# A dense table streamed by one transfer of 128 KB per step into a ring of eight, instead of 512 KB per four steps into a ring of four

## The chip, the cores and the metric

The kernel runs on one core of one Trainium2 chip. The metric is the device time of a run in microseconds. PE is TensorE, DVE is VectorE, ACT is ScalarE, POOL is GpSimd, and SP is the sync engine, which here does nothing but issue transfers.

## The reference, cut to what matters

The model is a token mixer, a gated recurrent layer in both directions, and then a product-key attention over 16 sequences (batches) of 375 positions. Only the last stage touches the change. There, each position scores two lists of 64 keys per head, keeps 16 of each, takes the best 16 of their sums out of 4096 combinations, and sums the 16 chosen rows of a table with softmax weights:

```python
sim = jnp.einsum('pbnhd,pkhd->pbnhk', q, pk_keys)
scores, idx = jax.lax.top_k(sim, PK_TOPK)
...
final_scores, pk_idx = jax.lax.top_k(score, FINAL_TOPK)
final_scores = jax.nn.softmax(final_scores, axis=-1)
...
k = jnp.einsum('bnhk,bnhkd->bnhd', kv_scores, keys_table[ind])
v = jnp.einsum('bnhk,bnhkd->bnhd', kv_scores, values_table[ind])
```

A causal attention with these k and v and an output projection follow. Everything is float32 at the outputs.

## The kernel before, in words

The first 1090 us hold the mixer, the recurrence and its output. The rest is `attention` (line 740). It treats four heads by gathering: POOL issues 3024 indirect transfers of 128 rows (line 937), and PE sums the rows. The other four heads (DH = 4) are dense: the weights of all 4096 combinations are made on the chip and multiplied with the whole table. A batch is STEPS = 64 steps, 16 per dense head, and a step handles two chunks of 128 table rows:

- `exponent` (line 987): PE forms the exponents of 2 x 128 rows by 375 positions in banks 0 and 1, and ACT takes the exponential into `ex` (line 1203);
- `ranks` (line 1012): PE forms the sums that tell whether a row is chosen, and DVE compares and multiplies into `w` (line 1526);
- `product` (line 1020): PE multiplies two 128 x 128 tiles of the table, `dtab`, with `w`, adding in bank 4. In float32 each of the two shows as two weight loads and two matmuls in the trace, so a product is four of each.

PE's order within a step is written out in `step` (line 1107): the exponents of the next step, the product of the step before, the ranks of the next step, then other work by a table of places (`places`, line 656): attention scores, gathered rows, transposes. DVE, ACT and POOL run their own orders, tied to PE's by semaphores. All of it stands in one loop over batches 1 to 14, with batch 0 and 15 written out before and behind it (`run`, line 833).

The dense table in HBM holds 2 MB per head, 8 MB in all, and is read again for every batch. `dtab` (line 770) is a ring of SLOTS = 4 buffers of PIECE = 8 chunks, 4 KB per partition each, 16 KB in all; a piece is 512 KB and serves four steps. In the program of SP (line 888), `piece` (line 892) issues one such transfer, and `batch` (line 901) waits on `s_main`, which counts finished products, until the four steps of a buffer are done, and then refills it. SP has two other waits on the same queue: at a batch's start `h_now` (lines 902 and 903) waits for the promotion of the next rows (`s_cur`), and `row` (lines 905 and 906) waits for the fourth exponent of the batch (`s_X`); the store of the output of the batch before (line 909) comes between pieces. On PE, the product of every fourth step waits for its piece (line 1022) and, as all products do, for `w` (line 1023).

Which wait goes with which piece is a matter of three expressions:

```python
SLOTS = 4; PIECE = 8                                     # chunks in a piece
sp.wait_ge(s_main, n * STEPS + 4 * (i + 1))              # line 911, i in 0..15
pe.wait_ge(s_piece[p // 4 % SLOTS], n * (16 * DH) + 16 * (p // 4 // SLOTS + 1))   # line 1022
```

Of the kernel before, what the change touches and what calls it, by code (L numbers as in the profile page):

```python
# [15 lines left out]
T = (T_IN - 1) // STRIDE + 1  # L16
# [25 lines left out]
DH = H - GH  # L42
CHUNKS = NK * NK // 128
HALF = CHUNKS // 2
STEPS = DH * HALF
PIECE = 8
SLOTS = 4
HEADS = NT * H
LEN = 15

# [689 lines left out]
def attention(nc, cst, keymat, halves, table, dense, minus, hu, out, ps):  # L740
# [10 lines left out]
    with ExitStack() as ctx:  # L751
        BF16 = mybir.dt.bfloat16

        def sb(name, shape, dt=F32):
            return ctx.enter_context(nc.sbuf_tensor(name, shape, dt))

        def sem(name):
            return ctx.enter_context(nc.semaphore(name))
# [10 lines left out]
        left = sb("left", [128, 2, T])  # L769
        dtab = sb("dtab", [128, SLOTS, PIECE * 128])  # L770
        half = sb("half", [128, HALVES_WIDTH], BF16)
        ex = sb("ex", [128, 2, 2, T])
        w = sb("w", [128, 2, 2, T])
# [41 lines left out]
        s_row, s_h = sem("c_rows_loaded"), sem("c_residual_loaded")  # L815
        s_piece = [sem(f"c_piece_loaded{i}") for i in range(SLOTS)]
        s_cur = sem("c_row_promoted")
        s_X, s_D, s_ex, s_w, s_main, s_acc = (sem(n) for n in ("d_exponent", "d_rank_sum", "d_exp", "d_weight", "d_product", "d_head_copied"))
# [68 lines left out]
        @block.sync  # L887
        def _(sp):
            def row(b):
                sp.dma_start(u_front[0:64, :], hu[1, bass.ds(b, 1)].rearrange("o d t -> (o d) t")).then_inc(s_row, 16)  # L890

            def piece(i):
                h, part = i // 4, slice((i % 4) * PIECE * 128, (i % 4 + 1) * PIECE * 128)
                sp.dma_start(dtab[:, i % SLOTS, :], dense[h, :, part]).then_inc(s_piece[i % SLOTS], 16)

            def store(n):
                sp.wait_ge(s_osb, n)
                dst = out[bass.ds(n - 1, 1)].rearrange("o (c t) d -> t (o c) d", c=NT)
                sp.dma_start(dst, osb[:]).then_inc(s_out, 16)

            def batch(n, kind):
                sp.wait_ge(s_cur, n + 1)
                sp.dma_start(h_now[:], hu[0, bass.ds(n, 1)].rearrange("o d t -> (o d) t")).then_inc(s_h, 16)
                if kind != "last":
                    sp.wait_ge(s_X, n * STEPS + AHEAD)
                    row(n + 1)
                for i in range(4 * DH):
                    if i == 11 and kind != "first":
                        store(n)
                    if not (kind == "last" and i + SLOTS >= 4 * DH):  # L910
                        sp.wait_ge(s_main, n * STEPS + 4 * (i + 1))
                        piece((i + SLOTS) % (4 * DH))

            sp.dma_start(kdup[64:68], minus.rearrange("r h (j k) -> r h j k", j=2)).then_inc(s_kdup, 16)
            row(0)
            for i in range(SLOTS):
                piece(i)
            batch(0, "first")
            with sp.Fori(0, B - 2) as i:
                batch(i + 1, "mid")  # L920
            batch(B - 1, "last")
            store(B)
            sp.wait_ge(s_out, 16 * (B + 1))
# [19 lines left out]
        def _(pe):  # L943
            def mm(out_, lhsT, rhs, start=True, stop=True, open_bank=False):
                return nc.tensor.matmul(out_, lhsT, rhs, start=start, stop=stop, skip_group_check=open_bank)  # L945
# [72 lines left out]
                last.then_inc(s_D, 1)  # L1018

            def product(n, p):  # L1020
                if p % 4 == 0:
                    pe.wait_ge(s_piece[p // 4 % SLOTS], n * (16 * DH) + 16 * (p // 4 // SLOTS + 1))
                pe.wait_ge(s_w, n * STEPS + (p + 1))
                if p % HALF == 0:
                    pe.wait_ge(s_acc, n * DH + (p // HALF + 1))
                for j in range(2):
                    at = (p % 4) * 2 + j
                    last = mm(ps[:, 4, 0:T], dtab[:, (p // 4) % SLOTS, at * 128:(at + 1) * 128], w[:, p % 2, j, :],
                              start=(p % HALF == 0 and j == 0), stop=(p % HALF == HALF - 1 and j == 1))
                last.then_inc(s_main, 1)  # L1030

# [75 lines left out]
            def step(p, kind, n):  # L1107
                following = (n, p + 1) if p + 1 < STEPS else (n + 1, 0)
                dense = kind != "epilogue" and not (kind == "last" and p + 1 == STEPS)
                if dense:  # L1110
                    if p + 1 == STEPS:
                        ready(n + 1, kind)
                    exponent(*following)
                if p >= 1 and kind != "epilogue":
                    product(n, p - 1)
                if p == 0 and kind != "first":
                    product(n - 1, STEPS - 1)
                if dense:
                    ranks(*following)
                for name, i in here(0, p, kind) + here(1, p, kind):  # L1120
                    if name == "sim":
                        sim(i, kind, n)
                    if name == "query":
                        query(i, kind, n)
                    if name == "value":
                        value(i, kind, n)
                    if name == "turn_probs":
                        turn_probs(i, kind, n)
                    if name == "part" and i >= 2:
                        part(i, kind, n)  # L1130
                    if name == "eat":
                        gathered(i, kind, n)
                for m in items(TURN_AT, p - 1, kind):
                    weigh(m, kind, n)
# [531 lines left out]
```

## Time and profile before

| what | us |
|---|---|
| median of 3 runs | 7210.47 |
| lowest and highest of them | 7197.34, 7213.68 |
| the profiled execution, its own time | 7216.25 |
| its span, first to last instruction | 7214.4 |
| mean granted TensorE clock in it | 0.765 |

The rows further down come from the one profiled execution; its time is 5.8 us above the median of the runs. The span is 1.9 us shorter than that execution's time. Busy time is that of an engine's own instructions; waits, register operations and the issue of transfers are not busy time. "PEld" is the weight load, which overlaps PE's matmuls. "Idle before" of a group is the idle time of the engine just ahead of its instructions, and "<-" names what ended most of it ("issue": nothing that the profile shows; "remote": a release whose origin it does not show). Line 945 is a helper through which all matmuls of this stage go, so that they are told apart by their tiles.

### The profile page before, as it was taken

Reading aid. Unit: us, or ns where it says so; the run is one execution under the profiler, and the core shown is the slowest. Engines: PE = TensorE matmul, PEld = TensorE weight load, DVE = VectorE, ACT = ScalarE, POOL = GpSimd, SP = SyncE. Lnnn points to the kernel's source line nnn. Section 1 sums busy time; section 2 is a strip of 40 time slices with the busy share of each in tenths; the row PEclk is TensorE's granted clock in tenths of the full one; section 3 lists DMA queues with packets and bytes.
Section 4 is the critical chain, followed back from the end, with each engine's and each line's share of the span. In section 5 each row is a group of like instructions: output and inputs, shape, how many; then the busy total and the mean of one; then the engine's idle time right before and its main releaser. Section 6 shows DMA issues by size and latency. Waiting matters only on the chain.

```text
span 7214.4 us, 93389 instructions
## 1 busy us (share of the span) xinstructions
PE 5504.2 (76%) x24068; PEld 3410.1 (47%) x24068; DVE 4381.4 (61%) x16725; ACT 2250.2 (31%) x5719; POOL 3144.6 (44%) x3416
## 2 busy tenths in 40 slices
PE   4566671578887878787878788888788888888879
PEld 2344430345554545454545455454455555554546
DVE  6666656665666666666665656575757575756522
ACT  2333330223332323232323333333333233333323
POOL 0011103455555455555454545454555555555541
PEclk7555565778787878887878787888888878788877
DMA  1000001122122222221222122212122212221210
GB/s 32 0 0 0 0 12 51 46 56 59 55 62 57 60 57 62 57 61 52 61 56 61 55 59 57 61 56 63 54 61 56 61 53 61 57 60 54 59 56 23
DMA packets 157848, 353.82 MB, mean 49 GB/s; under 512 B 71716, under 2 KB 75812, under 8 KB 156968
## 3 DMA queue, kind: packets, MB, share of 16 engines
q0 software_dynamic: 96912, 200.25, 10.5%
q1 hardware_dynamic: 60440, 147.74, 6.7%
q8 instruction: 216, 3.54, 0.2%
q14 instruction: 280, 2.29, 0.1%
HBM read 345.04 MB, written 4.61 MB: 48 GB/s over the span
## 4 chain that ended last, share of the span: by engine, by line
PE 34%; another core or an unknown queue 19%; DVE 15%; issue 12%; ACT 4%; DVEq 0%; DMA 0%; ACTq 0%; POOLq 0%
PE ps L945 34%; DVE topi L1340 2%; DVE w L1526 2%; DVE top L1334 2%; ACT ex L1203 1%; DVE sc L1346 1%; DVE idxf L1502 1%; DVE hot L1493 1%; DVE hot L1498 1%; DVE left L1304 1%; DVE eq L1471 1%; DVE cs L1346 1%; DVE wmat L1518 1%; DVE eq L1463 0%
## 5 line engine op out<-in xcount | busy, mean ns | idle before, releaser
L937 POOL DMA_INDIRECT rows<-table_dram,idxT x3024 | 3060.5, 1012 | 2923.8 <-PE ps L945 1660.5
L1526 DVE SCALAR_TENSOR_TENSOR w<-ps,ex 128x750 f32<-128x750 f32 x1024 | 958.8, 936 | 1950.1 <-remote 912.7
L945 PE MATMUL ps<-w,dtab 128*128 128x375 f32 x4096 | 1837.6, 580 | 5.5 <-issue 5.4
L945 PEld LDWEIGHTS ps<-w,dtab 128*128 128x128 f32 x4096 | 920.0, 232 | 486.0 <-issue 259.7
L1203 ACT ACTIVATE ex<-ps 128x750 f32<-128x750 f32 x1024 | 818.5, 799 | 716.6 <-PE ps L945 386.7
L945 PE MATMUL ps<-rank_dense,half 128*128 128x375 bf16 x1920 | 539.8, 368 | 493.6 <-DVE w L1526 346.0
L945 PEld LDWEIGHTS ps<-wmat,rows 128*128 128x128 f32 x6048 | 786.5, 207 | 138.9 <-issue 87.3
L945 PE MATMUL ps<-wmat,rows 128*128 128x8 f32 x6048 | 790.7, 265 | 57.8 <-issue 41.5
L945 PE MATMUL ps<-parts,half 128*128 128x375 bf16 x2048 | 611.7, 374 | 261.0 <-ACT ex L1203 169.7
L945 PEld LDWEIGHTS ps<-rank_dense,half 128*128 128x128 bf16 x1920 | 186.2, 109 | 1010.4 <-DVE w L1526 518.7
L1217 ACT COPY kvg<-ps 128x28 f32<-128x28 f32 x432 | 80.0, 185 | 1378.3 <-remote 823.6
L384 PE MATMUL ps<-h_moving,early 128*64 128x32 f32 x2250 | 316.3, 297 | 241.9 <-DVE h_moving L477 241.9
L384 PEld LDWEIGHTS ps<-h_moving,early 128*64 128x64 f32 x2250 | 266.3, 218 | 433.5 <-DVE h_moving L477 433.4
L945 PE MATMUL ps<-dg,prob 125*125 125x125 f32 x1536 | 316.9, 339 | 167.1 <-ACT kvg L1218 79.5
L945 PEld LDWEIGHTS ps<-parts,half 128*128 128x128 bf16 x2048 | 201.3, 117 | 427.6 <-ACT ex L1203 196.8
L945 PEld LDWEIGHTS ps<-dg,prob 125*125 125x125 f32 x1536 | 245.4, 228 | 284.0 <-issue 260.4
L491 POOL COPY states<-n_h 64x32 f32 (+1 forms) x375 | 76.6, 204 | 677.5 <-DVE n_h L480 677.5
L1244 ACT COPY probT<-ps 125x125 f32<-125x125 f32 (+2 forms) x384 | 141.9, 370 | 609.3 <-PE ps L945 331.0
L945 PE MATMUL ps<-kvT,qt 64*125 64x125 f32 (+2 forms) x768 | 293.3, 465 | 47.8 <-ACT vout L1227 31.6
L1340 DVE FIND_INDEX8 topi<-top,sc 125x8 uint32<-125x64 f32 x1536 | 306.4, 220 | 38.3 <-issue 37.1
L945 PE MATMUL ps<-vout,probT 125*125 125x64 f32 x1536 | 286.7, 318 | 38.4 <-issue 30.9
L945 PEld LDWEIGHTS ps<-vout,probT 125*125 125x125 f32 x1536 | 241.5, 224 | 98.6 <-issue 80.8
(206 smaller groups left out, 7015.4 us busy)
## 6 DMA issues: line engine op xcount, KB each, us to landing
dtab<-dense_dram SPq DMA_DIRECT2D x256, 512.0 KB
rows<-table_dram,idxT POOLq DMA_INDIRECT x3024
xin<-x_dram SPq DMA_DIRECT2D x16, 187.5 KB
half<-halves_dram POOLq DMA_DIRECT2D x1, 1828.0 KB, 13.0
rows_in<-hh SPq DMA_DIRECT2D x16, 93.8 KB, 2.2
rows_in<-uu SPq DMA_DIRECT2D x16, 93.8 KB, 2.2
u_front<-rows_in SPq DMA_DIRECT2D x16, 93.8 KB
h_now<-rows_in SPq DMA_DIRECT2D x16, 93.8 KB
```

The source lines that it names most:

```text
L384: return nc.tensor.matmul(out_, lhsT, rhs, start=start, stop=True, skip_group_check=True)
L491: nc.gpsimd.tensor_copy(states[:, bass.ds(s, 1), :].rearrange("p o b -> p (o b)"), after[:, k, 1::2]).then_inc(s_kept, 1)
L937: nc.gpsimd.indirect_dma_start(out=rows[:, t, :], out_offset=None, in_=table[:, :], in_offset=bass.IndirectOffsetOnAxis(ap=idxT[:, c, t:t ...
L945: return nc.tensor.matmul(out_, lhsT, rhs, start=start, stop=stop, skip_group_check=open_bank)
L1203: nc.scalar.activation(ex[:, p % 2, :, :], ps[:, 0:2, 0:T], ACT.Exp).then_inc(s_ex, 1)
L1217: nc.scalar.copy(kvg[:, :, c * TT + t0:c * TT + t1], src[:, 0])
L1244: nc.scalar.copy(probT[:, m % 2, 0:J], ps[0:TT, 6, 0:J]).then_inc(s_empty[1], 1)
L1304: nc.vector.tensor_tensor(left[64:128, half, :], ps[64:128, 5 + half, 0:T], parts[64:128, h % 2, half, :], ALU.subtract).then_inc(s_empty[ ...
L1334: last = nc.vector.max(best[:, g, 8 * half:8 * half + 8], values[:, g, :])
L1340: last = nc.vector.max_index(where[:, g, 8 * half:8 * half + 8], best[:, g, 8 * half:8 * half + 8], values[:, g, :])
L1346: last = nc.vector.match_replace(values[:, g, :], best[:, g, 8 * half:8 * half + 8], values[:, g, :], LOWEST)
L1526: nc.vector.scalar_tensor_tensor(w[:, p % 2, :, :], ps[:, 2:4, 0:T], float(K), ex[:, p % 2, :, :], ALU.is_gt, ALU.mult).then_inc(s_w, 1)
```

## The change

The piece becomes 2 chunks (128 KB, 1 KB per partition) and serves one step. The ring has 8 buffers, 8 KB per partition in all, half of before. SP waits for every product and issues 64 transfers a batch instead of 16; the store of the output still comes once product 44 of the batch is done. Every product on PE waits for its own piece. At the start SP fills eight buffers of 128 KB instead of four of 512 KB. The bytes moved in all are the same.

```diff
--- before.py
+++ after.py
@@ -43,8 +43,8 @@
 CHUNKS = NK * NK // 128
 HALF = CHUNKS // 2
 STEPS = DH * HALF
-PIECE = 8
-SLOTS = 4
+PIECE = 2
+SLOTS = 8
 HEADS = NT * H
 LEN = 15
 
@@ -890,7 +890,7 @@
                 sp.dma_start(u_front[0:64, :], hu[1, bass.ds(b, 1)].rearrange("o d t -> (o d) t")).then_inc(s_row, 16)
 
             def piece(i):
-                h, part = i // 4, slice((i % 4) * PIECE * 128, (i % 4 + 1) * PIECE * 128)
+                h, part = i // HALF, slice((i % HALF) * PIECE * 128, (i % HALF + 1) * PIECE * 128)
                 sp.dma_start(dtab[:, i % SLOTS, :], dense[h, :, part]).then_inc(s_piece[i % SLOTS], 16)
 
             def store(n):
@@ -904,12 +904,12 @@
                 if kind != "last":
                     sp.wait_ge(s_X, n * STEPS + AHEAD)
                     row(n + 1)
-                for i in range(4 * DH):
-                    if i == 11 and kind != "first":
+                for i in range(STEPS):
+                    if i == 44 and kind != "first":
                         store(n)
-                    if not (kind == "last" and i + SLOTS >= 4 * DH):
-                        sp.wait_ge(s_main, n * STEPS + 4 * (i + 1))
-                        piece((i + SLOTS) % (4 * DH))
+                    if not (kind == "last" and i + SLOTS >= STEPS):
+                        sp.wait_ge(s_main, n * STEPS + (i + 1))
+                        piece((i + SLOTS) % STEPS)
 
             sp.dma_start(kdup[64:68], minus.rearrange("r h (j k) -> r h j k", j=2)).then_inc(s_kdup, 16)
             row(0)
@@ -1018,14 +1018,12 @@
                 last.then_inc(s_D, 1)
 
             def product(n, p):
-                if p % 4 == 0:
-                    pe.wait_ge(s_piece[p // 4 % SLOTS], n * (16 * DH) + 16 * (p // 4 // SLOTS + 1))
+                pe.wait_ge(s_piece[p % SLOTS], n * (16 * STEPS // SLOTS) + 16 * (p // SLOTS + 1))
                 pe.wait_ge(s_w, n * STEPS + (p + 1))
                 if p % HALF == 0:
                     pe.wait_ge(s_acc, n * DH + (p // HALF + 1))
                 for j in range(2):
-                    at = (p % 4) * 2 + j
-                    last = mm(ps[:, 4, 0:T], dtab[:, (p // 4) % SLOTS, at * 128:(at + 1) * 128], w[:, p % 2, j, :],
+                    last = mm(ps[:, 4, 0:T], dtab[:, p % SLOTS, j * 128:(j + 1) * 128], w[:, p % 2, j, :],
                               start=(p % HALF == 0 and j == 0), stop=(p % HALF == HALF - 1 and j == 1))
                 last.then_inc(s_main, 1)
 
```

## Rows read from the trace of the kernel before

**Rows 1.** The page, parts 1 and 2: busy time of engines, granted clock in forty slices.

```profile
PE 5504.2 (76%) x24068; PEld 3410.1 (47%) x24068; DVE 4381.4 (61%) x16725; ACT 2250.2 (31%) x5719; POOL 3144.6 (44%) x3416
...
PEclk7555565778787878887878787888888878788877
```

**Rows 2.** The page, part 4: the chain that ended last, by engine.

```profile
PE 34%; another core or an unknown queue 19%; DVE 15%; issue 12%; ACT 4%; DVEq 0%; DMA 0%; ACTq 0%; POOLq 0%
```

**Rows 3.** The lines view, whole span: busy, mean of one, then idle before and its releaser.

```profile
L945 PE MATMUL ps<-w,dtab 128*128 128x375 f32 x4096 | 1837.6, 580 | 5.5 <-issue 5.4
L1526 DVE SCALAR_TENSOR_TENSOR w<-ps,ex 128x750 f32<-128x750 f32 x1024 | 958.8, 936 | 1950.1 <-remote 912.7 <-PE ps L945 497.5 <-ACT ex L1203 337.8
L945 PEld LDWEIGHTS ps<-w,dtab 128*128 128x128 f32 x4096 | 920.0, 232 | 486.0 <-issue 259.7 <-DVE w L1526 3.9 <-ACT kvT L1207 1.3
```

**Rows 4.** The waits view of PE: total, times, longest.

```profile
PE ps L945 <- DVE w L1526: 346.2, 170, 18.3
...
PE ps L945 <- ACT ex L1203: 171.3, 88, 9.8
```

**Rows 5.** One line each: 1023 and 1022, the waits of a product; minimum/median/maximum in ns.

```profile
L1023 PEldq EVENT_SEMAPHORE  x248: 51/51/51, 1330.9 to 7144.9; - x124
...
L1022 PEldq ALU_OP  x56: 32/32/32, 1668.3 to 6752.9; - x56
```

**Rows 6.** Timeline of weight loads, a step with a piece's wait, then one without.

```profile
3001.72 0.21 PEld L945 LDWEIGHTS ps<-parts,half 128*128 128x128 bf16 x2
3001.99 0.98 PEld L945 LDWEIGHTS ps<-w,dtab 128*128 128x128 f32 x4
...
3005.30 0.21 PEld L945 LDWEIGHTS ps<-parts,half 128*128 128x128 bf16 x2
3005.57 0.35 PEld L945 LDWEIGHTS ps<-w,dtab 128*128 128x128 f32 x2
```

**Rows 7.** Tile dtab on SP, whole span; then SP's timeline about one refill and a batch's start.

```profile
L894 SPq DMA_DIRECT2D dtab<-dense_dram x256: 327/328/654, 1092.8 to 7101.9; - x128
...
2999.95 25.24 SPq L894 DMA_DIRECT2D dtab<-dense_dram  x2
...
3149.38 0.47 SPq L890 DMA_DIRECT2D u_front<-rows_in  x1
```

**Rows 8.** The windows view about that refill: busy by engine, clock, DMA share, GB/s.

```profile
3000.70:3003.30 2.60, 2.60 (x18) 2.06 (x18) 2.54 (x12) 0.12 (x2) 1.90 (x2) 1.00 0.81 251
```

**Rows 9.** Tile dtab, last ten products; then product matmuls of a batch's start.

```profile
L945 PEld LDWEIGHTS ps<-w,dtab x40: 186/190/192, 7126.6 to 7151.7; 128*128 128x128 f32 x40
...
3146.01 1.43 PE L945 MATMUL ps<-w,dtab 128*128 128x375 f32 x4
...
3180.05 1.42 PE L945 MATMUL ps<-w,dtab 128*128 128x375 f32 x4
```

**Rows 10.** Queues and landings: hardware queue's share; small transfers' landing (tile rows_in).

```profile
q1 hardware_dynamic: 60440, 147.74, 6.7%
...
DMA to landing us min/median/max: 2.1/2.2/2.6
```

**Rows 11.** The chain about the start of this stage, and the windows view there.

```profile
1092.40 12.99 DMA half<-halves_dram
...
1092.00:1096.00 4.00, 0.00 (x0) 0.00 (x0) 1.26 (x6) 0.00 (x0) 0.74 (x1) 0.50 0.75 132
1096.00:1100.00 4.00, 0.00 (x0) 0.00 (x0) 0.00 (x0) 0.00 (x0) 0.00 (x0) 0.50 0.99 232
1100.00:1104.00 4.00, 0.00 (x0) 0.00 (x0) 0.00 (x0) 0.00 (x0) 0.00 (x0) 0.50 1.00 228
1104.00:1108.00 4.00, 2.57 (x3) 1.16 (x4) 0.18 (x1) 0.47 (x1) 0.00 (x0) 0.50 0.88 345
```

**Rows 12.** Windows of consecutive batches: the granted clock and busy time of each.

```profile
2786.00:3149.00 363.00, 290.50 (x1311) 181.58 (x1310) 230.12 (x888) 118.47 (x278) 190.75 (x189) 0.83 0.21 59
3149.00:3522.00 373.00, 300.12 (x1314) 186.51 (x1313) 231.16 (x888) 118.58 (x278) 192.17 (x189) 0.79 0.20 58
```

## The prediction

> **What bounds the kernel now.** I read the page first. Nothing is saturated: PE is busy for 76% of the span, DVE for 61%, POOL for 44%, and the granted clock of TensorE moves between 0.5 and 0.8 [rows 1]. The chain that ended last passes through PE for 34%, DVE for 15% and ACT for 4%; 19% is put down to releases that the profile doesn't show and 12% to issue. DMA has 0% of it [rows 2]. So the stage is a round of PE, ACT and DVE in which each waits for the others. Since POOL has no share, and the transfers none, a change of transfers can act only if it makes a wait or takes a wait away.
>
> Then I asked which waits a product meets. In the lines view PE sat idle for 5.5 us in all ahead of the 4096 matmuls that read dtab [rows 3]. That is the row to remember: over the whole kernel, product matmuls waited 5.5 us for everything together, table pieces included. DVE's multiplication into w in the same view stood idle for 1950.1 us before its 1024 instructions [rows 3]: the w side has slack, and PE's own long waits are for w and for ex (346.2 and 171.3 us), ahead of other matmuls [rows 4]. No wait of PE on dense_dram is to be found. The ring of four buffers hides its transfers wholly, and there is nothing here for finer pieces to gain.
>
> **The change part by part.** From the first u_front transfer inside the loop to the end of the stage the kernel does 64 steps in about 368 us: two consecutive batches took 363 and 373 us [rows 12], so a step is 5.75 us on average.
>
> *Waits on PE.* A product with a piece's wait carries two waits, and the trace shows what the second costs: it becomes an instruction of its own, 248 of them at line 1023, 51 ns each [rows 5]. (256 are in the program; a few records are missing.) The change gives such a pair to all 1024 products, 768 more. Line 1022 computes its four thresholds in registers, 4 in each of 14 loop turns, 56 at 32 ns [rows 5]; eight buffers make eight thresholds, 56 more, 56 x 32 = 1.8 us. If PE's sequencer lay bare all the time the cost would be 768 x 51 = 39.2 us, 41.0 us with the registers. That is one end. The other is nothing: in the timeline, the loads of a product with a piece's wait began 0.06 us after the load before them ended (3001.72 + 0.21 to 3001.99), and those of the next product, without it, also 0.06 us after (3005.30 + 0.21 to 3005.57) [rows 6]. The waits are taken while the two exponent matmuls ahead of the product are still running. Matmuls of the product sat idle 5.5 us over 1024 products [rows 3]; even if all of it belonged to the 256 with two waits, 768 more would cost 16.5 us. Per product it is 5 ns, and I take 768 x 5 ns = 4 us. A gain I exclude: an instruction is added and none goes.
>
> *Transfers, their number and price.* SP issues 1024 instead of 256, 0.327 us each [rows 7]: 335 us of SP in 7214 instead of 84. Per step that is 0.33 of 5.75 us, on an engine with nothing else to do; cover is the step itself. Cost nothing.
>
> *Transfers, how late a piece can be.* The 512 KB refill issued at 2999.95 [rows 7] kept the queues at 0.81 until 3003.30 [rows 8], so it is in the buffer 3.35 us after its issue. Transfers of 93.8 KB landed in 2.2 us [rows 10]. A 128 KB piece lies between, 2.2 to 3.35 us; its rows are 1 KB long rather than 4 KB, so I take 2.5. What has to cover it: buffer i is refilled when product i is done and wanted by product i + 8, which leaves seven steps where the old ring left twelve. On average that is 7 x 5.75 = 40 us. The shortest steps are at the end of the last batch: ten products, 40 weight loads from 7126.6 to 7151.7 [rows 9]; less 0.9 us for the last three loads that is 24.2 / 9 = 2.7 us a step, so seven steps are 19 us. Still more than five times the longest landing.
>
> *SP's queue is in order, and that bites at a batch's start.* Behind the 64th refill of a batch stand h_now's transfer and u_front's, with their waits for the promotion and the fourth exponent. u_front's was issued at 3149.38 [rows 7], while the batch's product 0 had begun at 3146.01 [rows 9]. So piece 8, due at about 3147.5, leaves at about 3149.9, some 2.4 us late. Product 8 began at 3180.05 [rows 9]: 30 us remain. Before, the next piece was due only after product 3, so nothing stood queued there. The store of the output sits behind product 44 in both versions. Cost nothing.
>
> *Contention.* The same bytes go as shorter pulses. During the 512 KB pulse all of PE's 2.60 us and 2.54 of 2.60 us of DVE were busy [rows 8]: nobody stalled. The hardware queue's packets have 6.7% of sixteen engines [rows 10]; even if every 1 KB row cost as much as two of its quarter shares, it would be 13%. Gain or loss by this: none that a row shows.
>
> *The first fill.* Here a transfer does stand on the chain: 12.99 us of `half`, 1828 KB, that shares the queues with the ring's first 2 MB [rows 11]. Moved from 1092 to 1104 were 4 x (132 + 232 + 228) = 2368 KB, and until 1105.4 some 1.4 x 345 = 480 KB more; less 1872 KB (1828 x 1.024) that leaves about 980 KB of table and rows. With a first fill of 1 MB the same 980 KB can still go ahead of the end of `half`. So nothing is gained; the bound would be 980 KB / 230 = 4.3 us if none of it competed.
>
> **Sum.** Against the profiled execution's 7216.25 us: + 4 (waits) + 0 + 0 + 0 = 7220. That execution is 5.8 us above the median of the runs, so the forecast is 7210.5 + 4 = 7214 us. Its own range is the bounds of the waits, 0 to 16.5, and the spread of the runs shown, 16 us: 7200 to 7230. A difference of 0.2%, 14 us, is about the least that a measurement of this kernel can tell from none.
>
> The Trainium skill speaks against this change: its page "DMA: Bandwidth & Descriptors", sections "Anatomy of one DMA" and "Bandwidth", gives a transfer a fixed 2.0 us plus bytes / 436 GB/s and asks to batch to 1 MB or more. By that a 512 KB piece takes 3.2 us and a 128 KB piece 2.3 us; the trace's 3.35 us agrees with the first, and no row here shows the second. By that rule the sum of the transfers' times would grow from 0.82 to 2.36 ms; whether that is paid is the third rival.
>
> **Rivals.** *First, slower: the added wait is not hidden.* Place: PE's sequencer ahead of product p, in the 768 steps that had no piece's wait. Price 51 ns each. It decides where PE comes starved to a step, having waited for ex, so that nothing is queued in front of the 51 ns. At half of the steps it is 20 us, 7231 to 7235; at all, 41 us, 7251. For it: PE waits for ex and w over 500 us [rows 4], so it is often starved. Against it: the 5.5 us [rows 3], and the equal gaps [rows 6], since two exponent matmuls always stand between the wait for ex and the product. Chance 0.17.
>
> *Second, either way: the rhythm moves TensorE's clock.* PE's 34% of the chain are 2450 us. Two consecutive batches with the same work had 0.83 and 0.79 granted and took 363 and 373 us [rows 12]. If the mean of 0.765 went by 0.01 to either side, this share would change by 1.3%, 32 us: 7182 or 7246. Nothing in the change aims at it, but each product now starts by another wait. Chance 0.13 up, 0.07 down.
>
> *Third, slower: pieces come late.* It decides where a landing takes over 19 us in the tail, or over 30 us behind the batch's start. If pieces were so late that each transfer lay bare, the cost would be 1024 x 2.2 less 256 x 3.35 = 1400 us, some 8600 us. Against it: landings of 2.2 and 3.35 us and the 0% of DMA in the chain [rows 2, 8, 10]. Chance 0.02. A small form of it, a few late pieces behind the batch's start, is 14 x a few us, inside the range.
>
> That the change doesn't do what it says is no rival: each transfer and each wait is written out.
>
> **How the numbers follow.** Forecast 0.61, waits bare 0.17, clock up 0.13 and down 0.07, late pieces 0.02. Faster by over 0.2% comes from the clock alone, and from it in all but a little: 0.13. Slower: 0.17 + 0.07 + 0.02 = 0.26, less the weaker half-bare cases that end under 14 us, plus the forecast's upper end: 0.25. Within: 0.62. The range reaches from part of the faster clock, 7188, to the slower clock and most of the bare waits, 7245; outside lie the full forms of both and the third rival.
>
> **What the changed profile would show.** Event semaphores at line 1023 of PE near 1024, 51 ns each; SP's issues of dtab 1024 at about 0.33 us; idle time before product matmuls still under 20 us; 1 KB rows on the hardware queue, with its share between 6.7 and 13%; no wait of PE on dense_dram; batches of 363 to 373 us. I am wrong if product matmuls show tens of us of idle time, if the mean clock differs by 0.01 or more, if a wait on dense_dram appears, or if SP's refills fall more than eight products behind.

## The result, and the profile after

The changed kernel took 7263.84 us in the median of nine runs, the kernel before 7206.46 us in nine: a ratio of 1.0083, with a 95% interval from 1.0058 to 1.0109. I had forecast 7214 us with a range up to 7245, and no difference as the likeliest case. It was slower, by 57 us, and outside the range. The profiled execution of the changed kernel has a span of 7284.2 us against 7214.4 before, 69.8 us more.

The page of the changed kernel (busy time, granted clock, hardware queue, the chain that ended last), against [rows 1, 2, 10]:

```profile
PE 5527.5 (76%) x24068; PEld 3422.0 (47%) x24068; DVE 4381.6 (60%) x16725; ACT 2248.6 (31%) x5719; POOL 3144.1 (43%) x3416
...
PEclk7555565778887878787878787878887888777877
...
q1 hardware_dynamic: 171032, 147.79, 6.8%
...
PE 33%; another core or an unknown queue 20%; issue 13%; DVE 13%; ACT 4%; DVEq 0%; DMA 0%; ACTq 0%; POOLq 0%
```

The packets of the hardware queue rose from 60440 to 171032, and their share only from 6.7 to 6.8%: that a table row is 1 KB instead of 4 KB cost the queues a tenth of a point. DMA has 0% of the chain, as before.

The lines view of the changed kernel (busy us, mean ns, idle before and its releasers), against [rows 3]:

```profile
L945 PE MATMUL ps<-w,dtab 128*128 128x375 f32 x4096 | 1849.6, 583 | 1.1 <-issue 1.1
L945 PEld LDWEIGHTS ps<-w,dtab 128*128 128x128 f32 x4096 | 926.8, 233 | 485.8 <-issue 266.2 <-ACT kvT L1205 3.0
L1524 DVE SCALAR_TENSOR_TENSOR w<-ps,ex 128x750 f32<-128x750 f32 x1024 | 960.3, 938 | 1981.0 <-remote 928.9 <-ACT ex L1201 425.4 <-PE ps L945 408.4
```

PE sat idle 1.1 us ahead of product matmuls instead of 5.5, and its weight loads 485.8 us ahead of products instead of 486.0 [rows 3]. The two places at which a bare wait or a late piece would show have not grown. DVE's w stood idle 31 us longer.

One line's view of the changed kernel, the second wait of a product (minimum/median/maximum in ns), against [rows 5]:

```profile
L1022 PEldq EVENT_SEMAPHORE  x1002: 51/51/51, 1321.8 to 7220.4; - x167
```

The tile view of dtab on SP in the changed kernel, against [rows 7]:

```profile
L894 SPq DMA_DIRECT2D dtab<-dense_dram x1024: 42/328/707, 1094.2 to 7200.7; - x171
```

Both are as the change has them: some 1000 waits of 51 ns, 1024 issues of 0.33 us at the median. Where then did 70 us go? The transfer of u_front is issued once before the stage and once in each of 15 batches, so that its first and last issue measure fifteen of them. The tile view of u_front on SP in the kernel before and then in the changed one:

```profile
L890 SPq DMA_DIRECT2D u_front<-rows_in x16: 468/474/518, 1092.2 to 6469.8; - x16
```

```profile
L890 SPq DMA_DIRECT2D u_front<-rows_in x16: 466/475/518, 1093.6 to 6532.2; - x16
```

5377.6 us before, 5438.6 after: 61 of the 70 us, 4.1 us a batch on average. By the single issues of u_front in the two traces, 11 of the 15 intervals are longer than before, by up to 12 us, and 4 are shorter, by up to 5 us: no one place carries the loss. The windows view of three batches of the changed kernel (each row: the stretch, its length, the busy time of PE, weight load, DVE, ACT and POOL, the granted clock, DMA share, GB/s), against [rows 12]:

```profile
3182.00:3550.00 368.00, 296.23 (x1312) 185.04 (x1311) 230.52 (x888) 118.60 (x278) 190.68 (x189) 0.82 0.21 58
3550.00:3920.00 370.00, 300.01 (x1311) 188.19 (x1311) 230.84 (x887) 119.38 (x278) 191.39 (x190) 0.82 0.21 58
6157.00:6532.00 375.00, 306.87 (x1312) 190.86 (x1311) 231.10 (x888) 118.88 (x278) 190.58 (x190) 0.79 0.21 57
```

Batches of 368 to 375 us with 0.79 to 0.82 of the clock, and DVE, ACT and POOL busy as before. No view names something new that is waited for.

### The profile page after: what moved, and what is told of

It is laid out like the page before. It is cut to its first block, busy times and chain, and to the rows that moved or that the text cites. A ratio compares the mean times of both kernels' runs of the same rounds, so it can differ in the third digit from the quotient of the medians.

```text
span 7284.2 us, 95653 instructions
## 1 busy us (share of the span) xinstructions
PE 5527.5 (76%) x24068; PEld 3422.0 (47%) x24068; DVE 4381.6 (60%) x16725; ACT 2248.6 (31%) x5719; POOL 3144.1 (43%) x3416
## 3 DMA queue, kind: packets, MB, share of 16 engines
q1 hardware_dynamic: 171032, 147.79, 6.8%
## 4 chain that ended last, share of the span: by engine, by line
PE 33%; another core or an unknown queue 20%; issue 13%; DVE 13%; ACT 4%; DVEq 0%; DMA 0%; ACTq 0%; POOLq 0%
PE ps L945 33%; DVE w L1524 2%; DVE topi L1338 2%; DVE top L1332 1%; ACT ex L1201 1%; DVE sc L1344 1%; DVE idxf L1500 1%; DVE hot L1491 1%; DVE eq L1469 1%; DVE left L1302 1%; DVE cs L1344 0%; DVE wmat L1516 0%; ACT prob L1232 0%; DVE fin L1332 0%
## 5 line engine op out<-in xcount | busy, mean ns | idle before, releaser
L1524 DVE SCALAR_TENSOR_TENSOR w<-ps,ex 128x750 f32<-128x750 f32 x1024 | 960.3, 938 | 1981.0 <-remote 928.9
L945 PEld LDWEIGHTS ps<-w,dtab 128*128 128x128 f32 x4096 | 926.8, 233 | 485.8 <-issue 266.2
## 6 DMA issues: line engine op xcount, KB each, us to landing
half<-halves_dram POOLq DMA_DIRECT2D x1, 1828.0 KB, 12.4
```

The source lines that it names most:

```text
L1524: nc.vector.scalar_tensor_tensor(w[:, p % 2, :, :], ps[:, 2:4, 0:T], float(K), ex[:, p % 2, :, :], ALU.is_gt, ALU.mult).then_inc(s_w, 1)
```

## The experiments

### First four: the addresses, the waits, the transfers

One thing in the changed trace pointed somewhere. The tile view of sc, strikes by DVE, in the changed kernel:

```profile
L1344 DVE MATCH_REPLACE8 sc<-top,sc x768: 206/221/271, 1116.2 to 6773.1; 125x64 f32<-125x64 f32 x192
```

The median was 209 ns before. The lines view has means of 224 ns for the strikes and 95 ns for the loads ahead of them, against 210 and 82 before; the 222 and 93 in the texts below are a little low. Since dtab shrank by 8 KB per partition, sc and everything behind it had moved. So the first suspect was the place of the tensors, with the waits and the number of transfers as rivals.

**e1, addresses kept.** To the changed kernel:

```diff
         dtab = sb("dtab", [128, SLOTS, PIECE * 128])
+        spare = sb("spare", [128, 2048])
```

> The changed kernel with an unused tensor of 8 KB per partition behind dtab, so that every later tensor keeps the address it had in the kernel before. In the trace of the changed kernel the strikes on sc (MATCH_REPLACE8) take 222 ns on average instead of 210 and the loads ahead of them 93 instead of 82, while the same operations on cs stay at 196 to 197. If the moved addresses cause that, the two means come back to 210 and 82 here. Theory of the addresses: the time too comes back, to within 0.3% of before (about 7210). Theory of the waits on PE, and that of the number of transfers: the time stays 0.7 to 0.9% above before (about 7260), whatever DVE's durations do.

Measured, in six runs: 7162.22 us against 7234.65, ratio 0.9898 (0.985 to 0.9946). Not back to before, but clearly faster than it. The changed kernel itself was not run beside it. The strikes were back at 210 ns on average.

**e2, addresses moved.** To the kernel before:

```diff
-        dtab = sb("dtab", [128, SLOTS, PIECE * 128])
+        spare = sb("spare", [128, 2048])
...
         osb = sb("osb", [TT, NT, D])
+        dtab = sb("dtab", [128, SLOTS, PIECE * 128])
```

> The kernel before with its own pieces, ring and waits, but dtab allocated last and an unused tensor of 8 KB per partition in its old place, so that all later tensors have the addresses of the changed kernel. Theory of the addresses: 0.5 to 0.9% slower than before (7245 to 7270), strikes on sc near 222 ns. Theory of the waits and of the transfers: same time as before within 0.3%. If DVE's durations do not change here either, they come from the traffic, not from the place.

Measured: 7234.56 us, ratio 0.9999 (0.9968 to 1.0029), and strikes of 210 ns. Moving the tensors alone shows no effect.

**e3, a wait at every product.** To the kernel before:

```diff
-                if p % 4 == 0:
-                    pe.wait_ge(s_piece[p // 4 % SLOTS], n * (16 * DH) + 16 * (p // 4 // SLOTS + 1))
+                pe.wait_ge(s_piece[p // 4 % SLOTS], n * (16 * DH) + 16 * (p // 4 // SLOTS + 1))
```

> The kernel before, but the wait for the piece stands ahead of every product instead of every fourth; it is already met in three of four. Event semaphores of that line rise from 248 to about 1000 records of 51 ns. Theory of the waits: 0.4 to 0.9% slower (7240 to 7270; 768 x 51 ns = 39 us is 0.54%). Theory of the addresses and of the transfers, and my prediction's own step: within 0.3% of before, + 4 us.

Measured: 7220.75 us, ratio 0.9983 (0.9953 to 1.0013). The 39 us of bare waits are excluded: the interval ends 9 us above before.

**e4, four transfers a piece.** To the kernel before:

```diff
-                sp.dma_start(dtab[:, i % SLOTS, :], dense[h, :, part]).then_inc(s_piece[i % SLOTS], 16)
+                for k in range(4):
+                    h, at = i // 4, (i % 4) * PIECE * 128 + k * 256
+                    sp.dma_start(dtab[:, i % SLOTS, k * 256:(k + 1) * 256], dense[h, :, at:at + 256]).then_inc(s_piece[i % SLOTS], 16)
...
-                    pe.wait_ge(s_piece[p // 4 % SLOTS], n * (16 * DH) + 16 * (p // 4 // SLOTS + 1))
+                    pe.wait_ge(s_piece[p // 4 % SLOTS], n * (64 * DH) + 64 * (p // 4 // SLOTS + 1))
```

> The kernel before, but each piece of 512 KB is issued as four transfers of 128 KB one after the other (rows of 1 KB in HBM and in SBUF, as in the changed kernel), with the ring, the addresses and PE's waits as before. 1024 transfers and four times the completions. Theory of the transfers: 0.4 to 0.9% slower (7240 to 7270), and the strikes on sc longer if completions or 1 KB rows disturb DVE. Theory of the addresses and of the waits: within 0.3% of before.

Measured: 7222.19 us, ratio 0.9975 (0.9944 to 1.0005). The number of transfers shows no cost either: the interval ends 0.05% above before. None of the three parts explained a loss, and the changed schedule came out as a gain in e1.

### Next four: another level

**e5, the changed kernel itself.** No edit.

> The changed kernel itself, unaltered, on the same chip as the three beside it. Before this, e1 (changed schedule, old addresses) was 1.0% faster than before, and e2 (old schedule, new addresses) equal to it; in both, the strikes on sc took 210 ns as before, while the changed kernel's trace had 222. Theory that moved addresses and the new ring only cost together: here 0.6 to 1.1% slower than before again, strikes on sc near 222 ns. Theory that the chip made the difference in durations: strikes near 210 ns, and the time between 0.99 and 1.00 of before, like e1.

**e6** has the edit of e1.

> e1 again, to know whether its gain of 1.0% repeats, beside the changed kernel. Theory of the addresses: 0.98 to 0.995 of before, and 1.3 to 2% under the changed kernel. If e1's gain was chance or of its chip: within 0.3% of before, or equal to the changed kernel.

**e7, a ring of sixteen.** To the changed kernel:

```diff
-SLOTS = 8
+SLOTS = 16
```

> The changed kernel with sixteen buffers of 128 KB instead of eight: 16 KB per partition in all, so the addresses of before with nothing unused, one transfer and one wait per product, and the lead of a refill 15 steps. Theory of the addresses: like e1, 0.98 to 0.995 of before. Theory that a shorter lead (seven steps) is what helps or hurts: differs from e6 by more than 0.4%.

**e8, pieces of two steps.** To the changed kernel (not shown: the refill loop runs over half as many pieces, each after two products, and the places in `dtab` follow):

```diff
-PIECE = 2
-SLOTS = 8
+PIECE = 4
+SLOTS = 4
...
-                pe.wait_ge(s_piece[p % SLOTS], n * (16 * STEPS // SLOTS) + 16 * (p // SLOTS + 1))
+                if p % 2 == 0:
+                    pe.wait_ge(s_piece[p // 2 % SLOTS], n * (8 * STEPS // SLOTS) + 16 * (p // 2 // SLOTS + 1))
```

> Pieces of 256 KB, one per two steps, in a ring of four: 8 KB per partition in all, so the addresses of the changed kernel, with half its transfers and waits (512 transfers, a second wait at 512 products). Theory of the addresses: as slow as the changed kernel, 0.6 to 1.1% over before. Theory of a cost per transfer or per wait: about half of the changed kernel's loss, 0.3 to 0.5%.

Here the kernel before, unaltered, took 5688.65 us in 35 runs, where it had taken over 7200. Against that: e5 5693.63 us (1.0022, 1.0000 to 1.0044), e6 5697.85 us (1.0019, 1.0004 to 1.0033), e7 5705.33 us (1.0028, 1.0011 to 1.0045), e8 5694.02 us (1.0006, 0.9991 to 1.0021). So there are two levels of time for one and the same program, about 7200 us and about 5690 us, below the slow and the fast level. e5 and e6 are equal, so the addresses make no difference at the fast one. e7 is 0.1% from e6, where the theory of the lead wanted over 0.4%. Whether the 0.2 to 0.3% of e5, e6 and e7 are a small steady cost was open; e8, with half the transfers and waits, had 0.06%, within its noise. In e5 the strikes on sc were as before the change (the tile view of sc in e5):

```profile
L1344 DVE MATCH_REPLACE8 sc<-top,sc x768: 199/209/221, 1115.1 to 5290.9; 125x64 f32<-125x64 f32 x192
```

The page of e5 and, in the second fence, its lines view:

```profile
PE 4910.3 (86%) x24068; PEld 3127.2 (55%) x24068; DVE 4355.3 (77%) x16725; ACT 2265.7 (40%) x5719; POOL 3200.5 (56%) x3416
...
PEclk7655555758999999999998999999999999999997
...
PE 47%; DVE 22%; issue 9%; ACT 2%; DVEq 0%; DMA 0%; ACTq 0%; POOLq 0%
```

```profile
L945 PE MATMUL ps<-w,dtab 128*128 128x375 f32 x4096 | 1607.3, 518 | 0.0
L1524 DVE SCALAR_TENSOR_TENSOR w<-ps,ex 128x750 f32<-128x750 f32 x1024 | 957.4, 935 | 717.9 <-PE ps L945 640.7 <-ACT ex L1201 62.0 <-issue 7.1
```

At the level of 7200 us the chain goes 19 to 20% through "another core or an unknown queue"; here that item is absent. DVE's w is idle 717.9 us instead of 1950.1 [rows 3], and its "remote" part, 912.7 us before, is gone.

### Third four: the small steady costs

**e9** is the changed kernel, **e10** has e1's edit, **e11** e3's, **e12** e4's.

> The changed kernel. The kernel before took about 7230 us beside e1 to e4 and 5689 us beside e5 to e8, with a granted clock of 0.77 and 0.85 in the profiles, so a ratio is only good beside others of its own level. If the level is that of 7200 us: theory of the addresses, 1.005 to 1.011 as first measured; theory that a shift of this size is a matter of the chip and of the rhythm that it imposes: anything between 0.99 and 1.01, and no steady distance from the next kernel. If it is that of 5690 us: 1.000 to 1.004 as in e5.

> The changed schedule at the addresses of before, beside the changed kernel. Level of 7200 us: theory of the addresses, 0.985 to 0.995 of before as in e1, and 1.3 to 2% under the changed kernel; theory of the rhythm: no such distance, the two within 0.4% of each other. Level of 5690 us: 1.000 to 1.004 by both theories.

> Old pieces and ring, a piece's wait at each product (768 more of 51 ns). Theory that the waits cost what is steady in the change: at the level of 5690 us 1.001 to 1.003 like e5, 6 to 17 us, that is 8 to 22 ns for each added wait, and e8 with 256 added waits had a third of it. Theory of the transfers: within 0.1% of before. At the level of 7200 us: between 0.995 and 1.002, as in e3.

> Old ring, addresses and waits, each piece in four transfers of 128 KB. Theory of the waits: at the level of 5690 us within 0.1% of before. Theory of the transfers (four times the completions, 1 KB rows): 1.001 to 1.003. At the level of 7200 us: between 0.994 and 1.001, as in e4.

The level of 5690 us again (before: 5697.49). e9 0.9999 (0.9982 to 1.0016), e10 1.0000 (0.9980 to 1.0020), e11 1.0005 (0.9989 to 1.0021), e12 0.9997 (0.9977 to 1.0016). The 0.2% of e5 did not repeat, and no interval reaches 0.25%. The view of the second wait in e11, and in the fence behind it the lines view:

```profile
L1022 PEldq EVENT_SEMAPHORE  x1016: 51/51/51, 1287.1 to 5620.7; - x170
```

```profile
L945 PE MATMUL ps<-w,dtab 128*128 128x375 f32 x4096 | 1600.9, 516 | 0.0
```

1016 waits are there, and PE was never idle ahead of a product matmul.

### Last six: the level of 7200 us once more

**e13** (the changed kernel) and **e14** (e1's edit):

> The changed kernel once more, for its distance from before at the level of 7200 us. In the traces at that level 372 of the 1021 recorded ends of a product are followed by their semaphore only over 1 us later; at the level of 5690 us 0 or 1 is. Theory that the change costs 0.8% where matmuls end late: 1.005 to 1.011 at the level of 7200 us. Theory that the first ratio was one draw of a rhythm that differs from chip to chip: within 0.5% of before, either side. At the level of 5690 us: 0.998 to 1.003.

> The changed schedule at the addresses of before, beside e13. Theory of the addresses: at the level of 7200 us 0.985 to 0.995 of before and over 1% under e13. Theory of the rhythm: within 0.5% of before and of e13. At the level of 5690 us: as e13.

Level of 5690 us a third time: e13 0.9988 (0.9971 to 1.0004), e14 0.9993 (0.9978 to 1.0009).

**e15** (the changed kernel), **e16** (e1's edit) and **e17**, a ring of two:

```diff
-SLOTS = 8
+SLOTS = 2
```

> The changed kernel again, for its distance from before at the level of 7200 us, should that level come up. Theory that the change costs 0.8% where product matmuls end late: 1.005 to 1.011. Theory of a rhythm that differs from chip to chip: within 0.5% of before. At the level of 5690 us: 0.998 to 1.003, as in e5, e9 and e13.

> The changed schedule at the addresses of before. At the level of 7200 us the theory of the addresses wants 0.985 to 0.995 of before and over 1% under e15, the theory of the rhythm within 0.5% of both. At the level of 5690 us: 0.998 to 1.003.

> The changed kernel with two buffers instead of eight, so that a refill leads its product by one step, 4.3 us on average at the level of 5690 us and 2.7 us at least. It shows from where a late piece decides. If a 128 KB piece is in its buffer 2.5 us after its issue, as I estimated, the one step covers it nearly always and the time stays within 1% of before, the loss coming from the batch's start, where SP's queue is blocked by two waits and piece 2 leaves late (16 times 2 to 3 us, 40 us, 0.7%). If small transfers take over 4 us in all, each of 1024 is late by part of a step: over 3% slower, and PE shows waits on dense_dram. Either way seven steps of lead are not what made the changed kernel slower.

The slow level (before: 7216.76). e15 7166.88 us, 0.9939 (0.9917 to 0.9961); e16 7162.16 us, 0.9932 (0.9907 to 0.9957); e17 7168.83 us, 0.9934 (0.9910 to 0.9958). Two findings. The changed kernel was faster than before by 0.6%, where the first result had it 0.8% slower. And e15 and e16, at new and old addresses on the same occasion, are 0.07% apart. With e2 that leaves no effect of addresses in sight at this level; so e1's gain was most likely the changed schedule's on that occasion, which no run there shows, since the changed kernel wasn't run beside e1. The lines view of e15:

```profile
L945 PE MATMUL ps<-w,dtab 128*128 128x375 f32 x4096 | 1818.6, 574 | 12.4 <-issue 12.4
L1524 DVE SCALAR_TENSOR_TENSOR w<-ps,ex 128x750 f32<-128x750 f32 x1024 | 958.4, 936 | 1853.4 <-remote 709.6 <-ACT ex L1201 435.5 <-PE ps L945 427.2
```

The w of DVE is idle 1853.4 us here and 1981.0 in the first changed trace, from the same program. The tile view of u_front on SP in e15 has fifteen batches in 5329.2 us, 109 us less than the first changed trace:

```profile
L890 SPq DMA_DIRECT2D u_front<-rows_in x16: 466/475/519, 1094.0 to 6423.2; - x16
```

e17 settles late pieces. The waits view of PE in e17 (total, times, longest):

```profile
PE ps L945 <- DMA dtab<-dense_dram: 5.3, 8, 0.8
```

With one step of lead, PE's matmuls waited 5.3 us in all for the table, in 8 places, its weight loads 8.8 us in 9, and the time was that of the ring of eight. At this level, with steps of 5.6 us on average, a piece of 128 KB is hidden by a single step. The ring of two was not run at the fast level.

**e18**, the changed kernel:

> The changed kernel a last time, for one more draw. At the level of 7200 us its ratio has been 1.008 (the first result) and 0.994 (e15), at the level of 5690 us 1.002, 1.000 and 0.999. Theory of a rhythm that differs from chip to chip: at the slow level any value from 0.99 to 1.01, at the fast one 0.998 to 1.003. Theory that the change gains by itself where matmuls end late, the first result being an outlier: 0.990 to 0.996 at the slow level. Theory that it costs there: 1.005 to 1.011.

Measured: 7246.58 us against 7201.99, ratio 1.0050 (1.0027 to 1.0072). The lines view of e18:

```profile
L1524 DVE SCALAR_TENSOR_TENSOR w<-ps,ex 128x750 f32<-128x750 f32 x1024 | 958.5, 936 | 1977.0 <-remote 936.7 <-PE ps L945 452.3 <-ACT ex L1201 422.6
```

The changed kernel is the slower one again. At the slow level the changed kernel itself has now been measured three times, at 1.0083, 0.9939 and 1.0050, with intervals that exclude one another's middles, while the strikes on sc took 209 to 210 ns on average both in e15 and in e18. The results number the chips of e1, e15 and e18 as 9, 10 and 7, those of e5, e9 and e13 as 9, 11 and 5; the first result has no number. Chip 9 showed both levels on two occasions; within a level each occasion has a chip of its own, so the runs don't tell a difference between chips from one between occasions. Over the four occasions at the slow level the kernel before moved from 7202 to 7235 us, 0.5%, and the changed schedule (with e1's spare tensor on one of them) from 7162 to 7264, 1.4%.

## Why the prediction was wrong, by its own steps

**The waits on PE: right.** 4 us were forecast between bounds of 0 and 41. e11 gives 1.0005 (0.9989 to 1.0021) at the fast level, which is 3 us between -6 and +12, and e3 excludes the 39 us at the slow one. The reading that the second wait runs under the exponent matmuls held: PE's idle time ahead of product matmuls was 1.1 us in the first changed trace, and 12.4 and 4.6 in those of e15 and e18.

**Transfers: right.** Number and row length (e4, e12) cost nothing beyond the noise of 0.2%, and landing (e17) nothing at the slow level. The third rival, late pieces, is excluded with room to spare: the changed ring leaves seven steps, and at the slow level one was enough. The Trainium skill's page "DMA: Bandwidth & Descriptors", section "Anatomy of one DMA", makes a 128 KB transfer 2.3 us, by a formula fitted to transfers issued from GpSimd, while the pieces are issued by SP. The trace of e5 agrees closely: from a piece's issue to the last of the sixteen updates of its semaphore the median is 2.2 us, over the 909 pieces whose updates can be told apart. That is also under my estimate of 2.5. The 1.5 ms by which that rule lets the transfers' times grow in sum were never paid. Even the delay behind a batch's start, which I had priced at 2.4 us of 30 and in e17 at up to 0.7%, did not show.

**Contention and the first fill: right as far as seen.** The landing of `half` took 12.4 us by the page of the changed kernel, against 12.99 before [rows 11].

**What failed: the sum had no term for the rhythm of the stage, and the second rival priced it too low.** The rhythm is the order in which PE, DVE and ACT wait for each other within the steps. The sum put it at nothing and took the spread of three runs of one kernel, 16 us, as the noise of a comparison. The second rival gave it 0.07 for slower and a price by the mean granted clock: 32 us, 0.4%, for 0.01 of clock. The first result was up by 57 us in the medians and by 70 in the profiled runs, with a clock of 0.763 against 0.765, which by that rule is 6 us. The nine runs of the changed kernel had 0.766 on average. In e18 the twelve runs and the seventeen of the kernel before beside them have the same mean clock, 0.7675, and are 45 us apart in the medians. e15 had 0.768 and e18 0.767 in their profiled runs, with spans of 7146.2 and 7245.3 us from one program.

Among the runs of one kernel the rule is of the right size (0.001 of clock goes with 2 to 8 us), but it doesn't carry the shift between the kernels. So the rival named the right kind of thing as far as the runs can tell, a shift that no single part sets, but not by the mean clock, and its size is 0.5 to 1% either way. My doubt about a steady cost at the parts was misplaced; the doubt about the rhythm was too small. None of the signs that I had set for being wrong came: no tens of us of idle time ahead of product matmuls, no 0.01 of clock, no wait on dense_dram. They watched the parts, and the loss was not there.

**And a view was read too trustingly.** I called the 5.5 us the row to remember. It is true of the starts of matmuls, but at the slow level the starts do not tell how long the matmuls take. The timeline of PE in the kernel before, then ACT's and DVE's of the same stretch:

```profile
2892.48 0.83 PE L945 MATMUL ps<-parts,half 128*128 128x375 bf16 x2
2893.10 2.32 PE L945 MATMUL ps<-w,dtab 128*128 128x375 f32 x4
2895.26 0.48 PE L945 MATMUL ps<-rank_dense,half 128*128 128x375 bf16 x2
2895.67 0.86 PE L945 MATMUL ps<-cst,kvT 64*125 64x64 f32 x6
2896.46 0.92 PE L945 MATMUL ps<-dg,prob 125*125 125x125 f32 x6
2901.68 0.81 PE L945 MATMUL ps<-parts,half 128*128 128x375 bf16 x2 [4.30 <-ACT ex L1203]
2902.28 2.71 PE L945 MATMUL ps<-w,dtab 128*128 128x375 f32 x4
2915.18 0.81 PE L945 MATMUL ps<-rank_dense,half 128*128 128x375 bf16 x2 [10.19 <-DVE w L1526]
```

```profile
2900.83 0.80 ACT L1203 ACTIVATE ex<-ps 128x750 f32<-128x750 f32 x1 [6.86 <-remote]
...
2915.64 0.32 ACT L1227 COPY vout<-ps 125x192 f32<-125x192 f32 x1 [13.49 <-remote]
2915.85 0.48 ACT L1244 COPY probT<-ps 125x375 f32<-125x375 f32 x1
```

```profile
2894.44 0.22 DVE L1340 FIND_INDEX8 topi<-top,sc 125x8 uint32<-125x64 f32 x1
2914.19 0.94 DVE L1526 SCALAR_TENSOR_TENSOR w<-ps,ex 128x750 f32<-128x750 f32 x1 [19.53 <-remote]
```

By the first, the value and probability products are over at 2897.4 (2896.46 + 0.92). But ACT copies the results of the value products at 2915.64, 13.49 us idle before it, and of the probability products at 2915.85; it had no other work. DVE waited 19.53 us for the rank matmul that PE began at 2895.26. By the semaphores' updates in the same trace, that rank matmul was signalled at 2914.16, not at 2895.74, where the profile has its end; the product ahead of it at 2909.27, not at 2895.42, and the exponent matmuls ahead of that at 2900.81, not at 2893.31. The granted clock doesn't account for it. The windows view of a part of that stretch has the full grant, 1.00 (columns as above):

```profile
2895.00:2901.50 6.50, 2.38 (x16) 1.59 (x14) 0.00 (x0) 0.67 (x1) 4.98 (x6) 1.00 0.20 51
```

And from the exponent's signal to the product's, 8.46 us passed over four product matmuls, which take 0.48 us each at the median by the profile and 0.99 at most (the tile view of dtab in the kernel before):

```profile
L945 PE MATMUL ps<-w,dtab x4096: 475/478/989, 1318.0 to 7152.1; 128*128 128x375 f32 x196
```

Over the stage, of the 1024 last matmuls of a product 373 had the next update of their semaphore more than 1 us after the end that the profile models; in e5 it is 1, in e11 none. (The traces of the slow level lack updates: 883 of this semaphore's are recorded here and 1024 in e5. So some of the 373 only miss their own; 230 of the recorded updates come over 1 us after every modelled end.) The rows that I took for idle engines were nearly all waits for PE: of the 3247 us of waits that the waits view of the kernel before puts down to "remote", 3176 are on semaphores that only PE's matmuls and weight loads update, and of the 1378 us of the chain in "another core or an unknown queue" 1352 are. I passed over these 19%: they were the largest item of the chain after PE, and I wrote only that the profile doesn't show them.

**What stays open.** Why matmuls are signalled late on some occasions, and whether and how the changed schedule makes them so more or less from one to the next. There is a trace of a link, not a proof: the waits put down to "remote" sum to 2986 us in e15, 3294 in the first changed trace and 3353 in e18, least in the trace that is fastest. The experiments vary waits, transfers, lead and addresses one at a time and find none that has a steady sign; none was run on the occasion of the first result, so the cause of its +0.8% is not shown. That the change as such costs 0.8% is contradicted by e15 (and by e1, e16, e17, which are the same schedule with other buffers), and at the fast level by three measurements within 0.25% of none. That strikes on sc took 224 ns in one trace out of the six of the changed kernel is not explained; DVE's busy time there, in which overlapping instructions count once, was 4381.6 us against 4381.4 before, so it did not lengthen DVE's work. None of the versions run was faster than the kernel before at both levels beyond noise.

## What to carry to other kernels

Finer transfers with a shorter ring cost nothing here as long as each refill led its use by more than its landing: 128 KB pieces landed in 2.2 us, one step of 5.6 us on average covered them, and the ring could shrink from 16 KB to 2 KB per partition with no loss against the ring of eight (shown at the slow level alone). When a large share of the chain is put down to an unknown releaser, look first whether results are consumed much later than the matmuls' modelled ends. Here that went with a time that depended on the occasion: one change, whose cost shows at no place of the trace, came out at -0.6, +0.5 and +0.8%. A verdict under 1% then needs pairs from several occasions, not a narrow interval from one.

## What the runs showed of the hardware that I had not expected

The kernel before took 7202 to 7235 us on some occasions and 5689 to 5698 us on others, 21% less, with all kernels of an occasion at the same level. The mean granted clock was 0.765 in the profile of the kernel before at the slow level and 0.854 in that of the changed kernel (e5) at the fast one. The clock alone is not the whole of it: both levels show 0.5 and 1.0 as the only grants, and at the slow level a matmul's signal came 18 us late, part of that time at the full grant. The first 1090 us of the kernel, where PE is busy for 0.4 to 0.7 of the time, took the same at both levels (the changed kernel issued its first transfer of u_front at 1093.6 us in the first trace and at 1092.5 in e5). Results numbered chip 9 appear at both levels (e1 to e4, e5 to e8), so the number alone does not decide it.
